# Experts on routed tokens only: slot tiles sorted by expert, rows scattered and results gathered through memory, one image later

## The chip, the cores and the metric

One core of a Trainium2 chip runs the whole program in one launch. TensorE (PE) multiplies matrices, VectorE (DVE) and ScalarE (ACT) work on tiles in the on-chip memory and evacuate PE's results, GpSimd (POOL) issues the indirect DMAs (a DMA whose row addresses come from a list of indices), SyncE (SP) issues the others. Each engine works through its own list of instructions in order and waits on semaphores for the others. The metric is the device time in microseconds (us), the median of the runs.

## What is computed

Eight images of 56 x 56 tokens with 64 channels pass four residual layers. Cut to what matters here:

```python
x = x + conv0(ln(x))        # xn = normalised tokens; y = relu(xn xn^T)^2 (x W), all 3136 x 3136 pairs of an image
t = x + moe(ln(x)):         # 16 experts, 128 hidden units, two per token
    probs = softmax(a @ gate_w + gate_b); top_probs, top_idx = top_k(probs, 2)
    dispatch = sum(one_hot(top_idx) * top_probs / sum(top_probs))
    hidden = silu(a @ w1[e]) * (a @ w2[e])       # the reference: every expert for every token
    out = sum_e (hidden @ w3[e]) * dispatch[e]   # 14 of 16 shares are zero
x = x + deform(ln(x))       # 3x3 deformable convolution: 9 taps, each from 4 corners at learnt offsets
x = x + ffn(x)              # only on the tokens with the largest routing weights (half of each image, less one)
```

## The kernel before, in words

An image's 3136 tokens lie in 25 tiles of 128 (the last has 64) and in 7 chunks of 512 (the last 64). `image(k)` runs through these stages on PE, DVE and ACT: the **mixer** (the layer `conv0`: `sims` multiplies tokens with tokens, ACT's relu and a square on DVE, L777, or ACT follow, `mix` multiplies with the mixed tokens; two halves with 14 steps j in all), then norm and gate (`gate`), then the **dense experts**. There the chunk's 512 tokens go through all 16 experts: `up` (four f16 products, since each weight is held as a high and a low half), a silu on ACT (L1379), `hidden` on DVE (L866), two experts' `down` products, the share of the token spread to channels by another product (`spread`), `scale_pair` (L862), and `collect`, transposes that add the pair to the sum in PSUM. At the end of each chunk the sum goes to the tokens (L884, L888).

Image k-1 is one layer further on beside it. Its deformable convolution takes corners from a table in memory: SP writes the table (`write_table`), and **POOL** walks through the images and their 25 tiles, with nine indirect gathers for each tile (L448: 128 rows of 1024 bytes) into a double buffer G. It waits for the table, for the indices, and until DVE has used the buffer of two tiles before (semaphore `valued`). DVE weighs a tile in five pieces (`weigh`: three products with the corner weights, L486, then two sums, L492 and L494), PE transposes and multiplies it (`sample`), ACT evacuates, DVE adds the result (`sample_add`, L499). Tuples at the top of the file say at which step of the mixer or at which expert a piece goes: ten tiles or so lie beside the mixers, 14 beside the experts, one beside the norm. Image k-2 has its FFN beside the same stages. After the loop come the last image's convolution alone, and the top-k that ranks all tokens.

All products and transposes but those of `sample` go through one helper, `mm`, so they carry its line, L1487.

Of the kernel before, what the change touches and what calls it, by code (L numbers as in the profile page):

```python
# [11 lines left out]
MOE_SAMPLE, MOE_EVAC, MOE_ADD, MOE_WEIGH = (0, 2, 4, 6), (2, 4, 6), 7, (1, 3, 4, 5, 7)  # L12

GEO_EVAC = ((1, 3), (1, 5), (1, 7), (2, 1), (2, 3), (2, 5), (2, 7))
# [5 lines left out]
FFN_EVAC = ((11, 1), (11, 3), (11, 5), (11, 7), (12, 1), (12, 3), (12, 5))  # L20

NORM_DVE, NORM_ACT = (0, 2, 6), (0, 3, 5)


def metaformer_kernel(nc, x, conv_w, gate_w, gate_b, w1, w2, w3, off_w, off_b, dcn_w, wr, br, f1, fb1, f2, fb2,
# [38 lines left out]
    NW = 6  # L64
    ACT_N = len(ACT_STEPS)
# [5 lines left out]
    grid_dram = nc.dram_tensor("grid_scratch", [N, 2 * TAPS], f32).ap()  # L71
    x3_dram = nc.dram_tensor("x3_scratch", [B, N, C], f32).ap()
# [3 lines left out]
    with ctx:  # L76
# [9 lines left out]
        pick = sb("pick", [128, E * C], f16)  # L86
# [8 lines left out]
        w1h = sb("w1h", [128, E * HID], f16)  # L95
        w1l = sb("w1l", [128, E * HID], f16)
        w2h = sb("w2h", [128, E * HID], f16)
        w2l = sb("w2l", [128, E * HID], f16)
# [27 lines left out]
        def routed(flat):  # L126
# [3 lines left out]
        xin_flat, xln_flat, x1_flat, yw_flat = (sb(n, [128, RT * C]) for n in ("xin", "xln", "x1", "yw"))  # L130
        xin, xln, x1, fc = tokens_of(xin_flat), tokens_of(xln_flat), tokens_of(x1_flat), tokens_of(yw_flat)
        yw = routed(yw_flat)
        xm = sb("xm", [TP, T, C])
        tmp = sb("tmp", [TP, T, C])
        xB = [sb(f"xB{q}", [TP, T, C]) for q in range(2)]
        st = sb("st", [TP, 3, 8, T])
        split = sb("split", [TP, T, 4 * C], f16)
        xn_hl = sb("xn_hl", [128, N], f16)
        xn_hh = sb("xn_hh", [128, N], f16)
        xn_ll = sb("xn_ll", [128, N], f16)  # L140
        xf = sb("xf", [128, N], f16)
        dT = xn_hh
# [3 lines left out]
        work = sb("work", [128, max(12 * IWM, 6 * 512 + RT * C)])  # L146
        relu = work[:, 0:4 * IWM].rearrange("p (q b n) -> p q b n", q=2, b=2)
        sq = work[:, 4 * IWM:12 * IWM].rearrange("p (q b n) -> p q b n", q=4, b=2)
        fin_x = (routed(x1_flat), routed(xin_flat))
        fin_y = (work[0:RP, 6 * 512:6 * 512 + RT * C].rearrange("p (t c) -> p t c", c=C), routed(xln_flat))  # L150
        silu = work[:, 0:2 * 512].rearrange("p (q n) -> p q n", q=2)
        hid = work[:, 2 * 512:6 * 512].rearrange("p (q n) -> p q n", q=4)
        small_all = sb("small", [128, 5, 2 * TAPS * T])
# [4 lines left out]
        disp = small[:, 4, 0:T * E].rearrange("p (t e) -> p t e", e=E)  # L158
        dsplit = sb("dsplit", [TP, T, 2 * E], f16)
        om = sb("om", [TP, T, OC])  # L160
        om_cm = sb("om_cm", [128, 512])
# [9 lines left out]
        share = small_flat[:, 0:2 * 512].rearrange("p (q n) -> p q n", q=2)  # L171
        scaled_y = small_flat[:, 2 * 512:4 * 512].rearrange("p (q n) -> p q n", q=2)
        w_all = sb("w_all", [RP, B, RT])

        hit = sb("hit", [RP, NTRY * (B - 1) * RT])
# [21 lines left out]
            logits_done sm_shift sm_exp disp_split disp_tr disp_cm  # L197
            up_done silu_done hid_done share_done share_ready down_done scaled_done ytm_done x2_added
# [5 lines left out]
        gath = (s["gath0"], s["gath1"])  # L204
        BODIES, GROUP = 2 * BPH, 14
        NLATE = T - FULL - 2 * NCH
# [89 lines left out]
        def late_tile(j):  # L296

            return FULL + 2 * NCH + j

        def moe_tile(c, i):  # L300

            return FULL + 2 * c + i

        def token_form(b, t):

            return b == LAST or FULL <= t < FULL + 2 * NCH

        def column_tiles(b, t):

            return b * (T - 2 * NCH) + (t + 1 if t < FULL else t + 1 - 2 * NCH)  # L310
# [3 lines left out]
        def _(sp):  # L314
# [16 lines left out]

            def store_x3(f):
                sp.wait_ge(s["skip_added"], 4 * (f + 1))
                sp.dma_start(whole_tiles(x3_dram[f]), xB[f % 2][:, 0:T - 1, :]).then_inc(s["x3_stored"], 16)
                sp.dma_start(last_tile(x3_dram[f]), xB[f % 2][0:REM, T - 1, :]).then_inc(s["x3_stored"], 16)
# [33 lines left out]
            sp.dma_start(stage3[0:2 * E, 1536:1536 + E * C], pick_in).then_inc(s["w_staged"], 16)  # L369
# [3 lines left out]
            for table in tables:  # L373
                tz = table.rearrange("e n -> (e n)").rearrange("(p n) -> p n", p=128)
                for a in parts:
                    sp.dma_start(tz[:, a:a + 1682], stage[:, 0:1682]).then_inc(s["table_zeroed"], 16)
            sp.wait_ge(s["table_zeroed"], 32 * len(parts))
# [6 lines left out]
            def image(k):  # L384
                if k >= 1:
                    write_table(k - 1)
                if k >= 2:
                    store_x3(k - 2)
                if k + 1 < B:
                    sp.wait_ge(s["x1_added"], 4 * (k + 1))  # L390
                    load_x(k + 1)
                if k >= 2:
                    store_yw(k - 2)

            for k in range(B):
                image(k)
            write_table(B - 1)
            store_x3(B - 2)
            store_yw(B - 2)
# [22 lines left out]
            sp.dma_start(whole_tiles(x3_dram[LAST]), xB[q][:, 0:T - 1, :]).then_inc(s["x3_stored"], 16)  # L422
            sp.dma_start(last_tile(x3_dram[LAST]), xB[q][0:REM, T - 1, :]).then_inc(s["x3_stored"], 16)
# [9 lines left out]
        @block.gpsimd  # L433
        def _(pool):
            pool.wait_ge(s["amax_done"], 1)
            GP.partition_all_reduce(amax_all[:, :], amax[:, :], 128, bass.bass_isa.ReduceOp.max).then_inc(s["amax_red"], 1)

            for b in range(B):
                pool.wait_ge(s["table_written"], (b + 1) * 64)
                for t in range(T):  # L440
                    if t in (0, GROUP):
                        pool.wait_ge(s["idx_ready"], 2 * b + 1 + t // GROUP)
                    n, rows = b * T + t, tile_rows(t)
                    if n >= 2:
                        pool.wait_ge(s["valued"], n - 1)
                    for tap in range(TAPS):
                        col = t * TAPS + tap
                        GP.indirect_dma_start(G[0:rows, n % 2, tap * 4 * C:(tap + 1) * 4 * C], None, tables[b % 2],  # L448
                                              bass.IndirectOffsetOnAxis(ap=index[0:rows, col:col + 1], axis=0)).then_inc(gath[n % 2], 16)
# [3 lines left out]
        def _(dve):  # L453
# [14 lines left out]
            def magnitudes(tensors):  # L468
                for col, src in tensors:
                    red(amax[:, col:col + 1], src, ALU.max)  # L470
                    red(amin[:, col:col + 1], src, ALU.min)
# [25 lines left out]
            def sample_add(b, t):  # L497
                dve.wait_ge(s["dcn_done"], b * T + t + 1)
                V.tensor_tensor(xB[b % 2][:, t, :], xB[b % 2][:, t, :], D0[0:TP, 448:448 + C], ALU.add).then_inc(s["conv_added"], 1)  # L499
# [32 lines left out]
            def split_l(ln, n, half, q):  # L532
                dve.wait_ge(s[ln + "_cast"], 4 * n + q + 1)
                h, r = half * 2 * C, quarter(q)
# [460 lines left out]
            for k in range(B):  # L995
                image(k)
# [926 lines left out]
```

## Time and profile before

| | |
|---|---|
| time, median of 3 runs (lowest to highest) | 4182.69 us (4178.13 to 4189.22) |
| the profiled execution: span | 4742.8 us, clock 0.858 |
| busy in it: PE, DVE, ACT, POOL | 3689.9, 3096.6, 2394.1, 1954.9 us |
| DMA | 314.93 MB in 374811 packets |

The profile's span is the profiled execution's own time as far as it is recorded; it is longer than the runs without the profiler. Busy times of different engines overlap. "Idle before" is the time in which an engine waited ahead of an instruction, and the arrow names what it waited for; "issue" stands for no wait that the profile shows and "remote" for a releaser that it cannot name.

### The profile page before, as it was taken

Reading aid. Unit: us, or ns where it says so; the run is one execution under the profiler, and the core shown is the slowest. Engines: PE = TensorE matmul, PEld = TensorE weight load, DVE = VectorE, ACT = ScalarE, POOL = GpSimd, SP = SyncE. Lnnn points to the kernel's source line nnn. Section 1 sums busy time; section 2 is a strip of 40 time slices with the busy share of each in tenths; the row PEclk is TensorE's granted clock in tenths of the full one; section 3 lists DMA queues with packets and bytes.
Section 4 is the critical chain, followed back from the end, with each engine's and each line's share of the span. In section 5 each row is a group of like instructions: output and inputs, shape, how many; then the busy total and the mean of one; then the engine's idle time right before and its main releaser. Section 6 shows DMA issues by size and latency. Waiting matters only on the chain.

```text
span 4742.8 us, 58643 instructions
## 1 busy us (share of the span) xinstructions
PE 3689.9 (78%) x21912; PEld 1953.7 (41%) x21912; DVE 3096.6 (65%) x4834; ACT 2394.1 (50%) x4144; POOL 1954.9 (41%) x1805
## 2 busy tenths in 40 slices
PE   6889868888788878889788888889788888864432
PEld 2334434444444444444444444444544444433421
DVE  5466457766677566766577567766577576664765
ACT  5656644466445654466445664456444664431210
POOL 0000344526255343535255353544345354446661
PEclk8999979999799978999799888989799988975555
DMA  3000222222122221222122221231222222233436
GB/s 99 8 1 1 73 59 60 65 66 79 51 65 68 70 72 57 67 73 71 51 65 66 70 77 55 64 86 51 55 71 72 71 71 57 60 89 89 111 97 125
DMA packets 374811, 314.93 MB, mean 66 GB/s; under 512 B 312672, under 2 KB 317024, under 8 KB 374528
## 3 DMA queue, kind: packets, MB, share of 16 engines
q0 software_dynamic: 85248, 231.33, 16.5%
q1 hardware_dynamic: 289280, 79.88, 7.9%
q8 instruction: 172, 2.82, 0.2%
q14 instruction: 111, 0.91, 0.1%
HBM read 279.30 MB, written 57.69 MB: 71 GB/s over the span
## 4 chain that ended last, share of the span: by engine, by line
PE 54%; DVE 14%; ACT 9%; another core or an unknown queue 9%; issue 7%; DVEq 3%; DMA 2%; POOL 2%; SPq 1%; ACTq 0%
PE PS L1487 49%; DVE work L866 3%; PE PS L1690 3%; DVEq L488 2%; ACT work L1379 2%; DVE G L492 2%; POOL G L448 2%; PE PS L1522 1%; ACT work L1308 1%; DVE G L486 1%; DVE st L454 1%; DVE small L862 1%; DVE work L777 1%; DMA out<-x 1%
## 5 line engine op out<-in xcount | busy, mean ns | idle before, releaser
L448 POOL DMA_INDIRECT G<-corner_table,index x1800 | 1954.3, 1086 | 2651.6 <-DVE value L494 1256.1
L1379 ACT ACTIVATE work<-PS,descale 128x512 f32<-128x512 f32 (+2 forms) x896 | 565.5, 633 | 638.0 <-PE PS L1487 510.6
L866 DVE SCALAR_TENSOR_TENSOR work<-PS,descale,work 128x512 f32<-128x512 f32 (+2 forms) x896 | 604.8, 681 | 385.0 <-ACT work L1379 276.1
L1308 ACT ACTIVATE work<-PS 128x768 f32<-128x768 f32 (+2 forms) x800 | 650.5, 823 | 374.3 <-PE PS L1487 251.0
L777 DVE TENSOR_TENSOR work<-work 128x768 f32<-128x768 f32 (+2 forms) x496 | 481.1, 973 | 440.2 <-PE PS L1487 280.3
L1487 PE MATMUL PS<-xn_hl,xn_hh 128*128 128x384 f16 (+2 forms) x1600 | 550.8, 345 | 121.8 <-ACT work L1308 76.3
L1487 PE MATMUL PS<-work,xm 128*64 128x400 f32 (+3 forms) x3200 | 642.1, 514 | 0.4 <-DVE work L777 0.4
L486 DVE TENSOR_TENSOR G<-G,corner_w 128x768 f32<-128x768 f32 x600 | 559.8, 951 | 55.9 <-DMA G<-corner_table,index 53.4
L1487 PE MATMUL PS<-xn_hl,xn_ll 128*128 128x384 f16 (+2 forms) x1600 | 546.7, 342 | 0.0
L1487 PE MATMUL PS<-work,w3s 128*64 128x384 f32 (+2 forms) x1792 | 466.8, 600 | 85.6 <-DVE small L862 80.8
L1487 PE MATMUL PS<-xn_hl,w1h 128*128 128x512 f16 (+2 forms) x896 | 331.1, 370 | 157.5 <-DVE work L866 131.3
L1385 ACT ACTIVATE small<-PS 128x512 f32<-128x512 f32 (+2 forms) x448 | 243.0, 542 | 253.1 <-PE PS L1487 195.8
L1487 PEld LDWEIGHTS PS<-xn_hl,xn_hh 128*128 128x128 f16 (+1 forms) x1600 | 160.7, 100 | 461.8 <-ACT work L1308 211.9
L1487 PE MATMUL PS<-xn_hl,w1l 128*128 128x512 f16 (+2 forms) x896 | 329.9, 368 | 0.0
L1487 PE MATMUL PS<-xn_hl,w2h 128*128 128x512 f16 (+2 forms) x896 | 328.3, 366 | 0.0
L1487 PE MATMUL PS<-xn_hl,w2l 128*128 128x512 f16 (+2 forms) x896 | 328.1, 366 | 0.0
L1487 PEld LDWEIGHTS PS<-work,xm 128*64 128x64 f32 (+1 forms) x3200 | 241.3, 139 | 200.8 <-issue 167.2
L862 DVE TENSOR_TENSOR small<-PS,small 128x512 f32<-128x512 f32 (+2 forms) x448 | 276.9, 618 | 55.0 <-PE PS L1487 34.6
L1232 ACT ACTIVATE val_cm<-PS 128x512 f32<-128x512 f32 x200 | 118.3, 592 | 329.0 <-PE PS L1522 241.5
L492 DVE TENSOR_TENSOR G<-G 128x1152 f32<-128x1152 f32 x200 | 271.8, 1359 | 18.1 <-issue 0.4
L1690 PE MATMUL PS<-ident,small 128*128 128x128 f32 x1600 | 262.3, 284 | 2.8 <-issue 1.8
L1337 ACT ACTIVATE work<-work 128x768 f32<-128x768 f32 (+3 forms) x304 | 259.7, 854 | 3.2 <-PE PS L1487 3.1
(258 smaller groups left out, 4959.1 us busy)
## 6 DMA issues: line engine op xcount, KB each, us to landing
G<-corner_table,index POOLq DMA_INDIRECT x1800
corner_table<-rows_scratch SPq DMA_DIRECT2D x32, 784.0 KB
corner_table<-G SPq DMA_DIRECT2D x8, 841.0 KB, 8.5
xin<-x SPq DMA_DIRECT2D x8, 768.0 KB, 5.3
rows_scratch<-xln SPq DMA_DIRECT2D x8, 768.0 KB
x_scratch<-xB SPq DMA_DIRECT2D x8, 768.0 KB
yw_scratch<-yw SPq DMA_DIRECT2D x7, 784.0 KB
x<-x_scratch SPq DMA_DIRECT2D x4, 784.0 KB
```

Of the source, the lines that this page charges most:

```text
L448: GP.indirect_dma_start(G[0:rows, n % 2, tap * 4 * C:(tap + 1) * 4 * C], None, tables[b % 2], bass.IndirectOffsetOnAxis(ap=index[0:rows, c ...
L486: V.tensor_tensor(g, g, bc(w, 2, C), ALU.mult)
L492: V.tensor_tensor(g[:, :, 0:2, :], g[:, :, 0:2, :], g[:, :, 2:4, :], ALU.add)
L777: V.tensor_tensor(sq[0:rows, u % 4, :, 0:n], relu[0:rows, u % 2, :, 0:n], relu[0:rows, u % 2, :, 0:n], ALU.mult).then_inc(s["sq_dve"], 1)
L862: V.tensor_tensor(scaled_y[:, p % 2, 0:w], Y0[:, 0:w], share[:, p % 2, 0:w], ALU.mult).then_inc(s["scaled_done"], 1)
L866: V.scalar_tensor_tensor(hid[:, e % 4, 0:w], S[2 + e % 2][:, 0:w], descale[:, MOE2:MOE2 + 1], silu[:, e % 2, 0:w], ALU.mult, ALU.mult).the ...
L1308: A.activation(relu[0:rows, u % 2, :, 0:n], PS[u % 2][0:rows, :, 0:n], ACT.Relu).then_inc(s["relu_done"], 1)
L1337: A.activation(sq[0:rows, u % 4, :, 0:n], relu[0:rows, u % 2, :, 0:n], ACT.Square).then_inc(s["sq_act"], 1)
L1379: A.activation(silu[:, e % 2, 0:w], S[e % 2][:, 0:w], ACT.Silu, scale=descale[:, MOE1:MOE1 + 1]).then_inc(s["silu_done"], 1)
L1385: A.activation(share[:, e // 2 % 2, 0:w], Y1[:, 0:w], ACT.Copy, scale=1.0 / XS).then_inc(s["share_ready"], 1)
L1487: return P.matmul(o, a, b, start=start, stop=stop, skip_group_check=True)
L1690: ins = P.matmul(D1[0:rows, n * 128:(n + 1) * 128], scaled_y[:, p % 2, n * TP:n * TP + rows], ident[:, :], start=p == 0 and n == 0, stop=p ...
```

## The change

The experts no longer see all tokens. For each image, `positions` (PE) and `route` (DVE) count by products with a triangle of ones where each token stands among those of its expert. Each expert's tokens get whole tiles of 128 **slots**; the 6272 pairs of token and expert need at most 64 tiles. POOL writes each token's row (f16, high and low half) to its two slots in memory (`scatter_rows`, 50 indirect DMAs per image), SP loads the slots, PE works on four slot tiles at a time (16 groups): `turn_over` transposes them, `expert_numbers` reads four expert numbers into PE's registers, `up` and `down` address the weights by them. SP stores the results, POOL gathers them back by token (`gather_results`, 50 indirect DMAs), and `combine` multiplies with the shares and adds. So each layer behind the experts is one image later, and ten units run in place of eight images: unit k has the mixer and gate of image k, the experts of k-1, and the sampling of k-2 and k-3. Behind each mixer come 19 **turns** (8 in the last unit). A turn weighs one tile and samples one; in turns 7 to 15 it also has two groups of slot tiles, and gate, routing, FFN and the next image's norm have turns of their own.

The `sims` products take their stationary operand from a copy that was the moving one, so two copies per image are made instead of three.

The core of the diff, with new functions that it calls:

```diff
+LATE, FIRST, COLUMN = 17, 16, (16, 22)
+
+LATE_WEIGH, LATE_SAMPLE = (7, 8, 9, 10, 11, 12), (0, 8, 9, 10, 11, 12)
+
+SLOTS, TAIL_SLOTS = 19, 8
+
+A_TURN, GATE_TURN, ROUTE_TURN, FFN_TURN, GEO_TURN, NORM_TURN, MOE_TURN, STAT_TURN, STACK_TURN = 2, 3, 5, 3, 6, 5, 7, 16, 16
+
+SCATTERS_FIRST, SCATTERS_PER_TILE = 26, 4
...
+            def load_slots(i):
+                sp.wait_ge(s["scattered"], 2 * T * 16 * (i + 1))
...
-            for b in range(B):
-                pool.wait_ge(s["table_written"], (b + 1) * 64)
+            def gather_tile(b, t):
...
+            def scatter_rows(i, n):
+                t, j = n // 2, n % 2
+                rows = tile_rows(t)
+                GP.indirect_dma_start(slots_dram, bass.IndirectOffsetOnAxis(ap=slot[0:rows, i % 2, j * T + t:j * T + t + 1], axis=0),
+                                      split_a[0:rows, t, :], None).then_inc(s["scattered"], 16)
+
+            def gather_results(i):
+                pool.wait_ge(s["y_stored"], PIECES * 16 * (i + 1))
                 for t in range(T):
...
+                    rows = tile_rows(t)
+                    for j in range(2):
+                        GP.indirect_dma_start(token_y[0:rows, j, t, :], None, y_dram,
+                                              bass.IndirectOffsetOnAxis(ap=slot[0:rows, i % 2, j * T + t:j * T + t + 1], axis=0)
+                                              ).then_inc(s["y_gathered"], 16)
+
+            def unit(u):
+                if valid(u - 2):
+                    gather_results(u - 2)
+                if valid(u - 1):
+                    pool.wait_ge(s["slots_ready"], u)
+                    for n in range(SCATTERS_FIRST if valid(u - 3) else 2 * T):
+                        scatter_rows(u - 1, n)
+                if valid(u - 3):
+                    for t in range(LATE, T):
+                        gather_tile(u - 3, t)
+                        if valid(u - 1):
+                            for n in scatters_after(t):
+                                scatter_rows(u - 1, n)
+                if valid(u - 2):
+                    for t in range(LATE if u - 2 < LAST else T):
+                        gather_tile(u - 2, t)
...
+            def combine(i, step):
+
+                g, x = share[:, i % 2, :, :], xq[i % 4]
+                if step == 0:
+                    dve.wait_ge(s["y_gathered"], 2 * T * 16 * (i + 1))
...
-            def experts_chunk(k, c):
...
+            def route(k):
...
+                tt(c, D1[0:TP, 0:T * E].rearrange("p (t e) -> p t e", e=E), bc(base, 1, T), ALU.add)
+                for j, o in enumerate((o1, o2)):
+                    tt(p, o, c, ALU.mult)
+                    rd(smallc[:, j, :], p, ALU.add)
+                V.tensor_copy(slot[:, k % 2, 0:T], smallc[:, 0, :])
+                V.tensor_copy(slot[:, k % 2, T:2 * T], smallc[:, 1, :]).then_inc(s["slots_ready"], 1)
...
+            def hidden(i, g):
+                n = i * GROUPS + g
+                dve.wait_ge(s["silu_done"], n + 1)
+                V.scalar_tensor_tensor(hid[:, g % 4, :], S[2 + g % 2][:, :], descale[:, MOE2:MOE2 + 1], silu[:, g % 2, :],
+                                       ALU.mult, ALU.mult).then_inc(s["hid_done"], 1)
...
+            def turn(k, r):
...
+                b, t = turn_weigh(k, r)
+                if turn_holds(k, b):
+                    for piece in range(5):
+                        weigh(b, t, piece)
+                b, t = turn_sample(k, r)
+                if turn_holds(k, b):
+                    sample_add(b, t)
...
+                if k < B and r == ROUTE_TURN:
+                    route(k)
...
+                for n in norm_pieces(r):
+                    if k + 1 < B:
+                        norm_piece(k + 1, n)
+                for g in moe_steps(r):
+                    if valid(k - 1) and 1 <= g <= GROUPS:
+                        hidden(k - 1, g - 1)
...
+            def up(i, g):
+
+                pe.wait_ge(s["slot_ready"], i * GROUPS + g + 1)
+                if g >= 2:
+                    pe.wait_ge(s["hid_done"], i * GROUPS + g - 1)
+                experts = expert_numbers(i, g)
+                for n, e in enumerate(experts):
+                    x = slot_cm[:, g % 2, n * TP:(n + 1) * TP]
+                    for h, l, o in ((w1h, w1l, S[g % 2]), (w2h, w2l, S[2 + g % 2])):
+                        mm(o[:, n * TP:(n + 1) * TP], of_expert(h, e), x, True, False)
+                        ins = mm(o[:, n * TP:(n + 1) * TP], of_expert(l, e), x, False, True)
                 ins.then_inc(s["up_done"], 1)
...
+            def of_expert(w, e):
+                return w[:, bass.ds(e, 1), :].rearrange("p a n -> p (a n)")
...
+            def turn(k, r, experts):
+                b, t = turn_sample(k, r)
+                if turn_holds(k, b):
                     for stage in range(4):
...
+                        sample(b, t, stage)
...
+                for g in moe_steps(r):
+                    if valid(k - 1):
+                        if g < GROUPS:
+                            turn_over(k - 1, g)
+                        if 1 <= g <= GROUPS:
+                            experts[g - 1] = up(k - 1, g - 1)
+                        if g >= 2:
+                            down(k - 1, g - 2, experts[g - 2])
```

On POOL's own list, an image before was its tiles in a row (`corner_table0` for even images, `corner_table1` for odd ones, x216 being 24 tiles of nine). Before, at the start:

```order
L436 ISA amax_all<-amax 128x6
L448 DMA G<-corner_table0,index 128x256 x216
L448 DMA G<-corner_table0,index 64x256 x9
L448 DMA G<-corner_table1,index 128x256 x216
L448 DMA G<-corner_table1,index 64x256 x9
```

After, from the end of image 0's tiles on, as one unit follows another (`shared` holds the gathered results, `slot_rows` are the slots in memory):

```order
L548 DMA G<-corner_table0,index 64x256 x9
L548 DMA G<-corner_table1,index 128x256 x153
L562 DMA shared<-slot_results,slot 128x64 x48
L562 DMA shared<-slot_results,slot 64x64 x2
L554 DMA slot_rows<-split_a,slot 8192x128 x26
L548 DMA G<-corner_table1,index 128x256 x9
L554 DMA slot_rows<-split_a,slot 8192x128 x4
```

Seventeen tiles of image 1 (x153, tiles 0 to 16) now have 50 result gathers and 26 scatters between them and its tile 17, and four more scatters follow each of the next tiles.

On PE, two experts of a chunk before, in a later image (`xn_hl` are the chunk's tokens, `w1h` to `w2l` halves of an expert's weights, `work` the hidden units, `pick` the share product, `ident,small` the collecting transposes, `ident,value` the sampling beside):

```order
L1487 MATMUL PS2<-work,w3s 64x512 x2
L1487 MATMUL PS2<-xn_hh,pick 128x512
L1690 MATMUL PS3<-ident,small 128x128 x4
L1487 MATMUL PS0<-xn_hl,w1h 128x512
L1487 MATMUL PS0<-xn_hl,w1l 128x512
L1487 MATMUL PS1<-xn_hl,w2h 128x512
L1487 MATMUL PS1<-xn_hl,w2l 128x512
L1522 MATMUL PS3<-ident,value 128x128 x4
L1487 MATMUL PS0<-xn_hl,w1h 128x512
L1487 MATMUL PS0<-xn_hl,w1l 128x512
L1487 MATMUL PS1<-xn_hl,w2h 128x512
```

After, the sampling at the head of a turn and the beginning of a group, each product with its own expert and 128 columns (`expert_of` holds the expert numbers, the ISA rows set registers, `work` are the slots, turned over):

```order
L1724 MATMUL PS3<-ident,value 128x128 x4
L1728 MATMUL PS3<-ident,value 128x128
L1689 MATMUL PS3<-dcn,val_cm 128x64 x5
L1921 TENSOR_LOAD expert_of
L1689 ISA
L1689 MATMUL PS0<-work,experts_w 128x128
L1689 ISA
L1689 MATMUL PS0<-work,experts_w 128x128
L1689 ISA
```

What had been four products of 512 columns for each of 16 experts is four of 128 columns for each slot tile, with a register instruction ahead of each.

## Rows read from the trace of the kernel before

**Rows 1.** The page: span, and busy time, share and count of each engine.
```profile
span 4742.8 us, 58643 instructions
...
PE 3689.9 (78%) x21912; PEld 1953.7 (41%) x21912; DVE 3096.6 (65%) x4834; ACT 2394.1 (50%) x4144; POOL 1954.9 (41%) x1805
```

**Rows 2.** The page: the chain that ended last, by engine.
```profile
PE 54%; DVE 14%; ACT 9%; another core or an unknown queue 9%; issue 7%; DVEq 3%; DMA 2%; POOL 2%; SPq 1%; ACTq 0%
```

**Rows 3.** Windows (us): width, busy of each engine (instructions), granted clock, DMA share, GB/s.
```profile
56.00:202.00 146.00, 143.66 (x802) 61.38 (x801) 61.97 (x85) 107.28 (x139) 0.00 (x0) 1.00 0.16 51
248.00:436.00 188.00, 174.07 (x903) 76.90 (x904) 121.34 (x207) 105.27 (x178) 0.00 (x0) 0.99 0.00 1
2335.00:2600.00 265.00, 223.46 (x1213) 111.17 (x1213) 199.83 (x304) 127.40 (x232) 132.48 (x126) 0.94 0.23 66
2600.00:2822.00 222.00, 195.36 (x1215) 97.72 (x1215) 134.79 (x192) 143.47 (x242) 102.06 (x90) 0.91 0.27 72
2822.00:2878.00 56.00, 33.13 (x312) 25.94 (x310) 31.45 (x59) 26.17 (x47) 9.15 (x10) 0.68 0.16 41
4268.00:4650.00 382.00, 165.74 (x770) 134.24 (x770) 235.15 (x407) 68.14 (x114) 252.24 (x225) 0.50 0.43 106
4650.00:4743.00 93.00, 17.63 (x77) 13.47 (x77) 53.12 (x147) 6.40 (x10) 0.00 (x0) 0.50 0.52 101
```

**Rows 4.** Groups by line: POOL's gathers (line, engine, operation, count | busy, mean ns | idle before).
```profile
L448 POOL DMA_INDIRECT G<-corner_table,index x1800 | 1954.3, 1086 | 2651.6 <-DVE value L494 1256.1 <-DVE index L667 731.8 <-issue 663.7
```

**Rows 5.** Waits of POOL: line, releaser, us in total, times, longest.
```profile
POOL G L448 <- DVE value L494: 1256.1, 135, 46.9
...
POOL G L448 <- issue: 663.7, 1659, 51.2
```

**Rows 6.** Timeline of POOL, last image: start, us, instruction, idle before.
```profile
4409.97 0.94 POOL L448 DMA_INDIRECT G<-corner_table,index  x1 [0.30 <-issue]
4411.22 3.57 POOL L448 DMA_INDIRECT G<-corner_table,index  x1 [0.30 <-issue]
```

**Rows 7.** Timeline of DVE in the same stretch.
```profile
4411.28 2.69 DVE L486 TENSOR_TENSOR G<-G,corner_w 128x768 f32<-128x768 f32 x3
```

**Rows 8.** Groups by line: three of the dense experts' instructions.
```profile
L866 DVE SCALAR_TENSOR_TENSOR work<-PS,descale,work 128x512 f32<-128x512 f32 (+2 forms) x896 | 604.8, 681 | 385.0 <-ACT work L1379 276.1 <-issue 99.3
...
L1487 PE MATMUL PS<-work,w3s 128*64 128x384 f32 (+2 forms) x1792 | 466.8, 600 | 85.6 <-DVE small L862 80.8 <-issue 2.5 <-DVE work L866 2.2
L1487 PE MATMUL PS<-xn_hl,w1h 128*128 128x512 f16 (+2 forms) x896 | 331.1, 370 | 157.5 <-DVE work L866 131.3 <-issue 17.7 <-ACT xn_hh L1426 7.6
```

**Rows 9.** Groups by line: weight loads and small products, nearest to the new ones.
```profile
L1487 PE MATMUL PS<-dcn,val_cm 128*128 128x64 f32 x1230 | 197.6, 299 | 56.5 <-ACT val_cm L1235 50.9 <-issue 5.7
L1487 PEld LDWEIGHTS PS<-dcn,val_cm 128*128 128x128 f32 x1230 | 189.7, 221 | 87.8 <-ACT val_cm L1235 68.4 <-issue 8.5
...
L1522 PE MATMUL PS<-ident,value 128*128 128x128 f32 x800 | 140.2, 304 | 140.9 <-DVE xB L499 111.5 <-DVE value L494 28.8 <-issue 0.6
...
L1487 PEld LDWEIGHTS PS<-xn_hl,w1h 128*128 128x128 f16 x896 | 96.2, 107 | 224.8 <-DVE work L866 180.0 <-issue 26.3 <-ACT xn_hh L1426 8.7
```

**Rows 10.** Groups by line: DVE work with two inputs in SBUF.
```profile
L486 DVE TENSOR_TENSOR G<-G,corner_w 128x768 f32<-128x768 f32 x600 | 559.8, 951 | 55.9 <-DMA G<-corner_table,index 53.4 <-issue 2.2
...
L777 DVE TENSOR_TENSOR work<-work 128x768 f32<-128x768 f32 (+2 forms) x496 | 481.1, 973 | 440.2 <-PE PS L1487 280.3 <-remote 82.7 <-ACT work L1308 61.1
...
L492 DVE TENSOR_TENSOR G<-G 128x1152 f32<-128x1152 f32 x200 | 271.8, 1359 | 18.1 <-issue 0.4
...
L494 DVE TENSOR_TENSOR value<-G 128x576 f32<-128x576 f32 x200 | 152.2, 761 | 19.0 <-issue 1.3
```

**Rows 11.** Timeline of POOL: a 64-row gather and the next image's first gather.
```profile
4246.99 0.90 POOL L448 DMA_INDIRECT G<-corner_table,index  x1 [0.30 <-issue]
4268.38 1.06 POOL L448 DMA_INDIRECT G<-corner_table,index  x1 [20.49 <-issue]
```

**Rows 12.** Waits of DVE: one line's wait for a releaser that isn't named.
```profile
DVE small L824 <- remote: 74.9, 6, 13.2
```

More of the change, by code:

```diff
@@ L452, in _ @@
+            pool.wait_ge(s["slots_zeroed"], 16 * 2 * PIECES)
+            for u in range(UNITS):
+                unit(u)
         @block.vector
@@ L846, in gate @@
-                V.tensor_tensor(o2, o2, bc(m2, 2, E), ALU.mult)
+                V.tensor_tensor(hot[:, 0:T * E].rearrange("p (t e) -> p t e", e=E), o1, o2, ALU.add).then_inc(s["hot_ready"], 1)
+            def route(k):
+                p, o1, o2, c = routing_views()
+                tiles_f, end, other, base = (ends[:, i, :] for i in range(4))
+                dve.wait_ge(s["pos_done"], k + 1)
+                V.tensor_scalar(counts_i[:, :], D1[0:TP, T * E:(T + 1) * E], float(TP - 1), None, ALU.add)
@@ L956, in _, with unit @@
+            def unit(k):
+                if k < B:
+                    mixer(k)
+                else:
+                    idle_mixer(k)
+                for r in range(turns(k)):
+                    turn(k, r)
             V.memset(table_cell[:, :], 0.0)
@@ L994, in _ @@
             rounds_prepare()
[L995 to L1004 removed]
+            for k in range(UNITS):
+                unit(k)
             def views(b0, nb):
@@ L1434, in _, with unit @@
+            def unit(k):
+                if k < B:
+                    mixer(k)
+                else:
+                    idle_mixer(k)
+                for r in range(turns(k)):
+                    turn(k, r)
             for n in range(6 * NCH):
                 norm_piece(0, n)
-            stacks(0, 0, 3 * NCH)
+            stacks(0, 0, 2 * NCH)
             act.wait_ge(s["w_loaded"], 16 * 16)
             act.wait_ge(s["const_done"], 1)
-            for k in range(B):
-                image(k)
@@ L1441, in _ @@
-            for j in range(BPH):
-                for u in range(SPB):
-                    geo_prepare(LAST, j, u)
-                    for stage in range(3):
-                        if j < NLATE and MIX_EVAC[stage] == u:
-                            sample_evac(PREV, late_tile(j), stage)
+            for k in range(UNITS):
+                unit(k)
             def tail_gelu(f, c):
@@ L1618, in mix, with beside_mixer, idle_mixer @@
                 ins.then_inc(s["mixed"], 1)
+            def beside_mixer(k, j, v):
+                if valid(k - 2):
+                    geo_prepare(k - 2, j - 7, v)
+                if valid(k - 4):
+                    ffn_prepare(k - 4, j, v)
+                for stage in range(4):
+                    if valid(k - 3) and j in LATE_SAMPLE and MIX_SAMPLE[stage] == v:
+                        sample(k - 3, late_sample(j), stage)
+            def idle_mixer(k):
+                for j in range(BODIES):
+                    for v in range(0, steps(j % BPH), 2):
+                        beside_mixer(k, j, v)
             def mixer(k):
@@ new lines, in turn, with unit @@
+                for g in moe_steps(r):
+                    if valid(k - 1):
+                        if g < GROUPS:
+                            turn_over(k - 1, g)
+                        if 1 <= g <= GROUPS:
+                            experts[g - 1] = up(k - 1, g - 1)
+                        if g >= 2:
+                            down(k - 1, g - 2, experts[g - 2])
+                if k + 1 < B:
+                    stacks(k + 1, *stack_turn(r))
+            def unit(k):
+                if k < B:
+                    mixer(k)
+                else:
+                    idle_mixer(k)
+                experts = {}
+                for r in range(turns(k)):
+                    turn(k, r, experts)
@@ L1805, in _ @@
+            stacks(0, 0, 2 * NCH)
             pe.wait_ge(s["w_loaded"], 16 * 16)
@@ L1809, in _ @@
                 mm(bank[:, max(IWS):512], zero16[:, 0:128], zero16[:, 0:512 - max(IWS)])
-            for k in range(B):
-                image(k)
+            for k in range(UNITS):
+                unit(k)
             def count(n, columns):
```

934 lines of the change are left out of this document (481 added, 453 removed).

## The prediction

> **What bounds the kernel now.** First the page's totals: over a span of 4742.8 us PE is busy 78%, DVE 65%, ACT 50%, POOL 41% [rows 1]. No engine is full, so the bound has to be found by stage, and the chain of waits names it: 54% of it is PE, 14% DVE, 2% POOL [rows 2]. Nine per cent of the chain has a releaser that the profile cannot name and 7% none at all; those two, 16% or some 760 us, matter below. Then the windows by stage. With nothing beside it the mixer takes 146 us and the dense experts 188 us of image 0, PE busy 98% and 93% of that. With gathers and sampling beside them they take 265 us (experts, image 4) and 222 us (mixer, image 5), and the norm, gate and FFN between them 56 us: a period of 543 us, which seven images repeat. The last image has its 25 tiles of sampling alone, 382 us at a granted clock of 0.50 (1.2 GHz), and top-k ends 93 us later [rows 3].
>
> Last POOL, whose one kind of instruction decides my forecast. 1800 indirect gathers take 1954.3 us, 1.086 us each, and are late because of the double buffer G or the index, not because POOL is full [rows 4, 5]. Inside one tile they follow at 0.95 us busy plus 0.30 us before the next, 1.25 us from start to start, to the hundredth; one gather lasted 3.57 us, exactly while three L486 multiplies ran on DVE [rows 6, 7]. At the mean a gather costs 1.086 + 0.30 = 1.39 us, a tile of nine 12.5 us, an image's 225 gathers 313 us: 58% of the period. POOL has room for 543 - 313 = 230 us an image.
>
> **What the change removes.** Each image has 112 expert passes over 448 to 512 tokens. Per pass PE does four up products of 0.37 us and two down products of 0.60, and DVE's L866 takes 0.68 [rows 8]. Over 896 passes that is 4 x 331 + 467 = 1791 us of PE and 605 of DVE, beside the share products, the evacuations on ACT and L862. So the whole stage of 265 us goes; its 14 tiles of sampling and the pieces of the next image's norm, which lay beside, stay and go to the new turns.
>
> **What it adds to PE, DVE and ACT.** Sixteen groups of four slot tiles: sixteen products of 128 columns, a quarter of a 512-column row (0.09 us) and each with its own weight load of 0.10 us [rows 9]. Beside each other the two give 16 x 0.10 = 1.6 us, one behind the other 3.1. Four down products, by the nearest f32 row 0.30 us with 0.22 of load, are 1.2 to 2.1; four turning transposes, by the 0.30 of an f32 one, 1.2 at most [rows 9]. A group is 3 to 6.4 us of PE. A turn has two groups and one sampling tile (five transposes by 0.30, five products by 0.30 and loads: 3 to 4.2 us), so 9 to 17 us; DVE has 5.0 us of weighing (3 x 0.95 + 1.36 + 0.76 [rows 10]), two hidden products and three small norm pieces, about 9 us. The register loads of four expert numbers, two per turn, have no row before; they lie between nothing (PE ahead of its inputs) and the 0.30 us of the nearest small f32 row, and I take nothing. For the turn I take the middle, 11 to 13 us: about as long as a tile's nine gathers.
>
> The Trainium skill, DMA: Bandwidth & Descriptors, gives a tensor_load a floor of about 600 ns; no run here shows one. By it the 128 loads would be 77 us of PE, an estimate, and felt only where PE is late.
>
> **What it adds to POOL, which is the term that decides.** Per image 50 scatters and 50 result gathers, so 325 indirect DMAs where there were 225. They have no row of their own: the low end is the undisturbed 1.25 us, the high end 1.43 (below), and 1.39 is the mean of the nearest row, a fair price since they move 128 rows each as the others do, and a gather of 64 rows takes 0.90 us, hardly less [rows 11]. The unit then has 325 x 1.39 = 452 us of POOL in a single queue, in the order gather results, scatter, late tiles, next tiles. Everything else of the unit is shorter: the mixer's 146 us alone, and 19 turns of about 12 us, 228 us, with the norm and gate inside the first of them, are 374 to 430. So the queue becomes the bound, and turns wait on G's nine gathers.
>
> How far DVE holds POOL back changes with that. The extra over 1.25 us is 0.14 us a gather, 252 us in all, while the two-input DVE work of L486, L492, L494 and L777 is 560 + 272 + 152 + 481 = 1465 us: 17% of it is felt with POOL issuing 2502 of 4743 us. If POOL issues nearly always, the share nearly doubles: 1.25 + 0.18 = 1.43 us. I take 1.41.
>
> **The sum, in the profile's own terms.** First tile of image 0: unit 0 has start 56, mixer 146 and turns without experts, 285 in all; unit 1 another 146, 60 of norm and gate and nine turns of 10: about 585; then 50 result gathers (70, the first four of fourteen mixer steps beside them), seven more steps of 10.4 (73), in which offsets and index are made, and the wait for the table, 20 in the tail of now [rows 11]: 748 us. From there 2600 - 150 = 2450 indirect DMAs are still to come: 2450 x 1.41 = 3455. POOL's waits: 40 in unit 2, 20 in each of six units while gate and routing hold DVE, and 60 for the last image's table: 220. After the last gather 94, as before. 748 + 3455 + 220 + 94 = 4517 us against 4742.8: 5% shorter.
>
> **From the profile to the clock.** The profiled execution is 13% longer than the median of 4182.69 us (a factor of 0.882), and the two are not stretched alike. POOL's 0.95 and 0.30 repeat to the hundredth, beside anything and alone, which looks like its own price; DVE's waits of up to 13 us on a releaser that the profile cannot name, 74.9 us in six of them at one line, look like the profiler's [rows 12], and the 760 us of such steps in the chain is more than the 560 us to be explained. If POOL keeps its price, only head, waits and end shrink: 660 + 3455 + 194 + 83 = 4392. If everything shrinks alike, 4517 x 0.882 = 3984. I stand nearer to the first, since part of POOL's 0.14 us of disturbance may be the recorder's: 0.6 x 4392 + 0.4 x 3984 = 4230 us, 1% slower.
>
> **Rivals.**
> - All of it shrinks with the profile, POOL too: 3984 us, 3900 to 4080. For it: 0.30 us between two DMAs with nothing to wait for may be a recorder's. Against: no spread in it, where the recorder's other marks spread by microseconds. Chance 0.27.
> - Slower: the turns set the pace, not POOL. Place: the nine turns with experts, where each product waits for its own register and weights and PE works at a granted clock of 0.5 to 0.7, as it does between the stages and in the tail [rows 3]. At the upper bounds, 17 us and two loads of 0.30, a turn is 17.6, 5.1 over the tile's 12.5; nine turns of seven units are 321 us on top of POOL's time, 4230 + 0.882 x 321 = 4513. It decides from a turn of 12.5 us. For it: the 9 to 17 range; against: loads lie beside products in the rows before. Chance 0.14.
> - Slower too: DVE shuts POOL out for all of its two-input work. Per unit 75 x 0.95 + 25 x 1.36 + 25 x 0.76 + 62 x 0.97 = 184 us; 325 x 1.25 + 184 = 590 us, longer than the 543 of now, and 2450 DMAs at 1.82 give 4459 + 1062 = 5521 in the profile's terms, 4870 shrunk. Against: the mean extra is 0.14 us, 17% of that. Chance 0.04. In the Trainium skill, SBUF — State Buffer, the box on the DVE-blocks-DMA trap and the section behind it (A bandwidth-pool intuition that's wrong) say that POOL writes DMA descriptors through a port pair that it shares with VectorE, that a two-port operation there locks it out meanwhile, and that a DMA of 620 ns then took some 3100 ns. The trace agrees in kind by the 3.57 us gather, and by the mean of 1.086 not in amount.
> - POOL is not the bound because results and scatters cost much less than a gather (their rows are 256 bytes, G's 1024): at 0.6 us a unit is 225 x 1.39 + 60 = 373, the other engines' 400 decide: 748 + 7.5 x 400 + 150 = 3898, shrunk 3440, in part 3700. Against: the 64-row gathers of the last tile cost nearly what the others do [rows 11], so size hardly counts. Chance 0.05.
>
> **How the numbers follow.** The forecast, POOL's queue at its own price, has a chance of 0.50, with 4230 as its time and 4090 to 4400 as its own range. 0.3% is what a measurement of this kernel can tell, so 4170 to 4195 is no change. Of the 0.50, 0.13 falls below, 0.06 within and 0.31 above. The shrinking rival gives 0.26 faster and 0.01 same, the cheap scatters 0.05 faster, the two slower rivals 0.18. Faster 0.44, same 0.07, slower 0.49. The range leaves out the extreme of each side: 3920 to 4520.
>
> **What would show it.** In the profile after: POOL busy well above half the span, its idle time before a DMA mostly 0.3 us, mean 1.05 to 1.13 us; DVE's wait for G grown to many hundred us; PE far below 78%; the granted clock lower in the turns; tiles 12 to 13 us apart in the turns, and units of about 460 us. Wrong, if POOL waits on DVE's value as long as now (turns decide), if the mean of the added DMAs is far from 0.95 to 1.1 us, or if the first gathers come much later than 748 us.

## The result, and the profile after

The kernel after takes 4419.5 us (4413.8 to 4427.3, four runs) against 4183.4 before: ratio 1.057, 95% interval 1.055 to 1.059. It is slower by 5.7%, where 1% was forecast (4230 us), inside the range of 3920 to 4520. The profiled execution is one of the four, 4427.3 us, and this time as long as the others.

The page after: span, busy times, and the chain by engine.

```profile
span 4425.5 us, 51603 instructions
...
PE 2910.2 (66%) x17810; PEld 1891.5 (43%) x17810; DVE 2435.6 (55%) x3747; ACT 1761.2 (40%) x2959; POOL 2925.6 (66%) x2608
...
POOL 43%; PE 23%; issue 13%; DVE 11%; ACT 4%; DMA 3%; DVEq 2%; SPq 1%; ACTq 0%; POOLq 0%
```

POOL went from 41% busy in [rows 1] and 2% of the chain in [rows 2] to 66% and 43%; PE's share of the span fell, and nothing else has become full. POOL's 66% is the whole queue, though: the pause of 0.30 us behind each DMA isn't counted as busy. Groups by line (line, engine, operation, count | busy, mean ns | idle before); L548 answers to L448 in [rows 4], L623 to L486 in [rows 10]:

```profile
L548 POOL DMA_INDIRECT G<-corner_table,index x1800 | 2029.3, 1127 | 681.6 <-issue 537.0 <-DVE value L631 111.8 <-DVE index L822 32.7
...
L623 DVE TENSOR_TENSOR G<-G,corner_w 128x768 f32<-128x768 f32 x600 | 541.5, 953 | 678.2 <-DMA G<-corner_table,index 678.1
...
L554 POOL DMA_INDIRECT slot_rows<-split_a,slot x400 | 485.1, 1213 | 335.1 <-DVE slot L1046 213.5 <-issue 121.5
...
L562 POOL DMA_INDIRECT shared<-slot_results,slot x400 | 410.1, 1025 | 349.5 <-DMA slot_results<-shared 227.8 <-issue 121.7
```

2600 DMAs take 2029 + 485 + 410 = 2924 us, 1.125 each; with the pause 1.425. POOL's waits answer to [rows 5] (us in total, times, longest):

```profile
POOL G L548 <- issue: 537.0, 1762, 0.3
POOL shared L562 <- DMA slot_results<-shared: 227.8, 1, 227.8
POOL slot_rows L554 <- DVE slot L1046: 213.5, 1, 213.5
...
POOL G L548 <- DVE value L631: 111.8, 37, 18.7
```

The wait for DVE's `value`, 1256 us before, is 112. The two large ones are single waits at the start: for the slots of image 0 (213 us) and for its results (228). What waits now is DVE, for G, 678 us (L623 above), where [rows 10] show 53 before. The first and last start of the sampling's gathers (durations as min/median/max):

```profile
L548 POOL DMA_INDIRECT G<-corner_table,index x1800: 897/949/4403, 720.5 to 4331.3; - x180
```

From 720.5 to 4331.3 us POOL issues 2450 DMAs: 2450 x 1.425 = 3491, and 112 of waiting, 3603 of 3611 us. So the span is 720 us of filling, a queue that hardly pauses, and 94 us at the end.

Where the other engines of a unit wait for the queue is seen on POOL's timeline at the start of unit 7, beside the last mixer (start, us, instruction, idle before): the last gather of image 4's tile 16, then 50 result gathers, 26 scatters, and the first gather of tile 17.

```profile
2870.36 0.95 POOL L548 DMA_INDIRECT G<-corner_table,index  x1 [0.30 <-issue]
2871.61 0.95 POOL L562 DMA_INDIRECT shared<-slot_results,slot  x1 [0.30 <-issue]
...
2938.81 0.91 POOL L562 DMA_INDIRECT shared<-slot_results,slot  x1 [0.30 <-issue]
2940.03 1.00 POOL L554 DMA_INDIRECT slot_rows<-split_a,slot  x1 [0.30 <-issue]
...
2980.27 1.07 POOL L554 DMA_INDIRECT slot_rows<-split_a,slot  x1 [0.31 <-issue]
2981.64 0.98 POOL L548 DMA_INDIRECT G<-corner_table,index  x1 [0.30 <-issue]
```

Tile 16 is done at 2871 and tile 17 begins at 2982, 110 us later. DVE comes to tile 17's weighing in the mixer's middle and waits, with the mixer's squares (L951) queued behind:

```profile
2979.51 0.98 DVE L951 TENSOR_TENSOR work<-work 128x800 f32<-128x800 f32 x1
2994.49 1.83 DVE L623 TENSOR_TENSOR G<-G,corner_w 128x768 f32<-128x768 f32 x2 [13.99 <-DMA G<-corner_table,index]
```

### The profile page after: what moved, and what is told of

Its sections match the earlier page's. It is cut to its first block, busy times and chain, and to the rows that moved or that the text cites. A ratio compares the mean times of both kernels' runs of the same rounds, so it can differ in the third digit from the quotient of the medians.

```text
span 4425.5 us, 51603 instructions
## 1 busy us (share of the span) xinstructions
PE 2910.2 (66%) x17810; PEld 1891.5 (43%) x17810; DVE 2435.6 (55%) x3747; ACT 1761.2 (40%) x2959; POOL 2925.6 (66%) x2608
## 4 chain that ended last, share of the span: by engine, by line
POOL 43%; PE 23%; issue 13%; DVE 11%; ACT 4%; DMA 3%; DVEq 2%; SPq 1%; ACTq 0%; POOLq 0%
POOL G L548 28%; PE PS L1689 22%; POOL shared L562 9%; POOL slot_rows L554 6%; DVE G L623 2%; DMA G<-corner_table,index 2%; DVE G L629 1%; DMA out<-experts_w 1%; DVEq L625 1%; DVE small L972 1%; DVE value L631 1%; PE PS L1724 1%; DVE st L590 1%; ACT small L1551 0%; DVE smallc L590 0%
## 5 line engine op out<-in xcount | busy, mean ns | idle before, releaser
L548 POOL DMA_INDIRECT G<-corner_table,index x1800 | 2029.3, 1127 | 681.6 <-issue 537.0
L623 DVE TENSOR_TENSOR G<-G,corner_w 128x768 f32<-128x768 f32 x600 | 541.5, 953 | 678.2 <-DMA G<-corner_table,index 678.1
L1689 PE MATMUL PS<-xn 128*128 128x400 f16 (+3 forms) x3200 | 647.9, 346 | 236.0 <-ACT work L1515 229.8
L951 DVE TENSOR_TENSOR work<-work 128x768 f32<-128x768 f32 (+2 forms) x496 | 479.7, 973 | 457.0 <-PE PS L1689 415.3
L554 POOL DMA_INDIRECT slot_rows<-split_a,slot x400 | 485.1, 1213 | 335.1 <-DVE slot L1046 213.5
L562 POOL DMA_INDIRECT shared<-slot_results,slot x400 | 410.1, 1025 | 349.5 <-DMA slot_results<-shared 227.8
L1689 PEld LDWEIGHTS PS<-xn 128*128 128x128 f16 (+1 forms) x3200 | 289.8, 101 | 666.4 <-ACT work L1515 389.2
L1689 PE MATMUL PS<-dcn,val_cm 128*128 128x64 f32 x1580 | 349.5, 378 | 57.9 <-ACT val_cm L1426 57.9
L1689 PEld LDWEIGHTS PS<-dcn,val_cm 128*128 128x128 f32 x1580 | 331.1, 297 | 85.5 <-ACT val_cm L1426 85.5
L629 DVE TENSOR_TENSOR G<-G 128x1152 f32<-128x1152 f32 x200 | 271.7, 1358 | 15.8 <-issue 0.4
L1689 PE MATMUL PS<-work,experts_w 128*128 128x128 f16 x2048 | 259.8, 280 | 12.5 <-issue 11.7
L1689 PEld LDWEIGHTS PS<-work,experts_w 128*128 x2048 | 209.7, 120 | 54.0 <-issue 23.0
L1689 PE MATMUL PS<-w3s,work 128*128 x1024 | 214.2, 379 | 21.2 <-DVE work L1058 21.0
L1689 PEld LDWEIGHTS PS<-w3s,work 128*128 128x128 f32 x1024 | 196.4, 286 | 33.1 <-issue 26.0
```

Source lines behind the costliest of these rows:

```text
L554: GP.indirect_dma_start(slots_dram, bass.IndirectOffsetOnAxis(ap=slot[0:rows, i % 2, j * T + t:j * T + t + 1], axis=0), split_a[0:rows, t, ...
L562: GP.indirect_dma_start(token_y[0:rows, j, t, :], None, y_dram, bass.IndirectOffsetOnAxis(ap=slot[0:rows, i % 2, j * T + t:j * T + t + 1], ...
L623: V.tensor_tensor(g, g, bc(w, 2, C), ALU.mult)
L629: V.tensor_tensor(g[:, :, 0:2, :], g[:, :, 0:2, :], g[:, :, 2:4, :], ALU.add)
L951: V.tensor_tensor(sq[0:rows, u % 4, :, 0:n], relu[0:rows, u % 2, :, 0:n], relu[0:rows, u % 2, :, 0:n], ALU.mult).then_inc(s["sq_dve"], 1)
L1689: return P.matmul(o, a, b, start=start, stop=stop, skip_group_check=True)
```

## The experiments

Theory A: POOL's queue is the bound of the kernel after, each indirect DMA costs about 1.43 us there whatever it moves, with or without the profiler, and the profile of before that I forecast from was stretched. Theory B: POOL's cost shrinks without the profiler, and the loss is in the turns, the ten units or the addressed weights. All kernels below but the last were timed once, in the profiled execution itself, so only differences far above 0.3%, the spread of the four runs of the kernel after, are read from them.

**The kernel before, recorded once more.** No edit.

> The kernel before, unchanged, profiled a second time. Its first profile had a span of 4743 us against 4183 without the profiler, while the kernel after shows 4426 against 4419. Theory A (the stretching is a property of recording this kernel, above all of PE's many instructions, and repeats): span again 4650 to 4800, with DVE and ACT waits on unnamed releasers of 200 us and more. Theory B (one bad recording): span near 4200, and then POOL's 0.95 and 0.30 us stand in it unchanged.

Measured: 4193.4 us, span 4191.6. The second of its theories held: the first recording was longer than the runs by 13%, this one isn't. The page of the second recording (span, busy, chain by engine):

```profile
span 4191.6 us, 58643 instructions
...
PE 3546.0 (85%) x21912; PEld 1920.7 (46%) x21912; DVE 3088.6 (74%) x4834; ACT 2401.7 (57%) x4144; POOL 2003.0 (48%) x1805
...
PE 60%; DVE 16%; ACT 9%; issue 4%; POOL 4%; DVEq 4%; DMA 2%; SPq 1%; ACTq 0%
```

The releaser without a name, 9% of the chain in [rows 2], is gone. Windows of the second recording, columns as in [rows 3]: mixer and experts of image 0 with nothing beside, then experts (image 4) up to the next mixer, then mixer with norm, gate and FFN (image 5).

```profile
56.00:202.00 146.00, 144.08 (x791) 61.46 (x791) 60.97 (x82) 106.14 (x138) 0.00 (x0) 0.98 0.16 51
249.00:437.00 188.00, 173.82 (x900) 76.64 (x901) 121.00 (x207) 105.76 (x179) 0.00 (x0) 0.99 0.00 1
2069.00:2296.00 227.00, 209.15 (x1213) 108.08 (x1213) 198.80 (x303) 128.19 (x231) 129.07 (x124) 0.98 0.26 75
2296.00:2539.00 243.00, 224.88 (x1525) 128.55 (x1526) 166.20 (x253) 169.73 (x289) 117.16 (x102) 0.90 0.29 77
```

The stages without gathers beside them are the same in both recordings, 146 and 188 us. Those with gathers took 265 and 222 + 56 = 278 us in [rows 3] and take 227 and 243 here: the period that the runs have is 470 us and not 543 (456 to 473 from an image's first tile to the next one's, up to image 6). POOL's line is nearly as it was in [rows 4], 1112 ns for 1086:

```profile
L448 POOL DMA_INDIRECT G<-corner_table,index x1800 | 2002.4, 1112 | 2052.0 <-DVE value L494 729.1 <-DVE index L667 686.0 <-issue 636.8
```

So POOL's price was read rightly and PE's stages were not. What stretched the first recording, the profiler or something else in that one execution, isn't known; it didn't recur in the other recordings that have runs to compare with (this one, the kernel after, the last experiment), and it wasn't tried further.

**Dense experts, with idle gathers added to POOL's queue.**

```diff
+                    for m in range(EXTRA_N if b < LAST else 0):      # EXTRA_N = 8
+                        if n:
+                            pool.wait_ge(extras[m], 16 * n)
+                        GP.indirect_dma_start(extra[0:rows, m, :], None, x.rearrange("b h w c -> (b h w) c"),
+                                              bass.IndirectOffsetOnAxis(ap=extra_i[0:rows, m:m + 1], axis=0)).then_inc(extras[m], 16)
```

> The kernel before with the dense experts as they were, and eight idle indirect gathers of 128 rows of 256 bytes behind each tile of images 0 to 6 (1400 in all, into a tile that nobody reads). Theory A (POOL's queue is the bound of the kernel after, and an indirect DMA costs 1.43 us there and here, with or without the profiler): 3200 DMAs in one queue from about 480 us on, 480 + 3200 x 1.43 + 94 = 5150 us, up to 5300 with waits. Theory B (the kernel after is slow by its turns, its ten units or its addressed weights, and an indirect DMA without the profiler costs 1.1 us or less): 480 + 3200 x 1.1 + 94 = 4090, so no more than 4183 to 4400.

Measured: 5195.3 us, 1011 more than before for 1400 DMAs. POOL's waits there, and its two groups of DMAs:

```profile
POOL G L455 <- issue: 662.1, 1781, 20.1
POOL G L455 <- DVE index L679: 483.0, 1, 483.0
POOL extra L460 <- issue: 426.7, 1400, 0.3
POOL G L455 <- DVE value L506: 69.6, 18, 7.9
```

```profile
L455 POOL DMA_INDIRECT G<-corner_table,index x1800 | 1921.6, 1068 | 1214.6 <-issue 662.1 <-DVE index L679 483.0 <-DVE value L506 69.6
L460 POOL DMA_INDIRECT extra<-x,extra_i x1400 | 1493.8, 1067 | 426.7 <-issue 426.7
```

POOL waits 70 us for DVE after its start, so its queue is the bound of this kernel as well, with all of the old experts and none of the new units. Theory A holds against B, which had nothing above 4400. That the time is within 1% of A's 5150 is partly luck. A DMA cost 1.367 us here (1.067 and the pause) and not 1.43, which is 200 us less on 3200 of them. A first gather at 527 us in place of 480, the 70 us for DVE and another 128 us in gaps of up to 20 us (662.1 - 1781 x 0.30), none of which the 5150 holds, made up for it.

**The kernel after without result gathers, and without scatters as well.**

```diff
             def gather_results(i):
                 pool.wait_ge(s["y_stored"], PIECES * 16 * (i + 1))
-                for t in range(T):
...
-                dve.wait_ge(s["y_gathered"], 2 * T * 16 * (i + 1))
+                dve.wait_ge(s["y_stored"], PIECES * 16 * (i + 1))
```

and in the second kernel `scatter_rows` is empty, with the waits for its DMAs put on `slots_ready`. So `combine` adds whatever lies in the results' tile, and in the second kernel the slots hold zeros; all other work is done.

> The kernel after without its 400 result gathers (combine adds what lies in the slots' tile in place of the tokens' results). Theory A (POOL's queue): 400 x (1.025 + 0.30) = 530 us less, 3890; up to 4000 if the other engines' path of a unit is longer than POOL's 275 x 1.43 = 393 us. Theory B (turns, units): 4300 to 4420.

> The kernel after without its 400 result gathers and without its 400 scatters; slots hold zeros, all else is done on them. Theory A: POOL's 225 x 1.43 = 322 us per unit are no longer the bound; the other engines' path of a unit, 374 to 430 us by the prediction's terms, is: 3450 to 3800 us, and POOL waits on DVE's value again by hundreds of us. Theory B (turns, units): 4300 to 4420.

Measured: 4055.9 us (364 less than after) and 3992.8 (427 less). Neither theory is right alone. POOL was the bound, since the first 400 DMAs bring 0.91 us each; but not all of their 1.33, and the next 400 bring only 63 us. POOL's wait for DVE's `value` in the first and its two largest waits in the second say why:

```profile
POOL G L548 <- DVE value L625: 230.0, 44, 22.6
```

```profile
POOL G L548 <- DVE index L813: 661.2, 1, 661.2
POOL G L548 <- DVE value L622: 601.9, 67, 75.2
```

112 us has become 230 and 602: POOL has room again, and the other engines' path of a unit, forecast at 374 to 430, now sets the pace. In the second kernel the first tiles of images 0 to 5 follow each other at 415 to 429 us; the 661 us are the wait for the first index, at the start. Even if moving rows had cost POOL nothing, the kernel would have come to 3993, 4.6% below before.

**DVE's products left out.** `weigh` without its three multiplications (L623), in the kernel after.

```diff
-                    V.tensor_tensor(g, g, bc(w, 2, C), ALU.mult)
+                    pass
```

> The kernel after without DVE's 600 two-input products in weigh (L623); the sums behind them stay. Theory A (those products shut POOL out while it writes descriptors): the gather's mean falls from 1.13 us to about 1.0, 1800 x 0.13 and a little on scatters and results, 220 to 300 us less, 4120 to 4200. Theory B (the extra over 0.95 us has another cause, such as memory traffic): POOL's means as before, and since POOL's queue is the bound, 4380 to 4420 although DVE has 541 us less to do.

Measured: 4223.2 us, 196 less. POOL's groups:

```profile
L548 POOL DMA_INDIRECT G<-corner_table,index x1800 | 1866.6, 1037 | 653.8 <-issue 541.0 <-DVE value L631 80.1 <-DVE index L822 32.7
L554 POOL DMA_INDIRECT slot_rows<-split_a,slot x400 | 478.8, 1197 | 334.8 <-DVE slot L1046 213.3 <-issue 121.5
L562 POOL DMA_INDIRECT shared<-slot_results,slot x400 | 401.2, 1003 | 349.4 <-DMA slot_results<-shared 227.8 <-issue 121.6
```

The gather fell from 1.127 to 1.037 us, 1800 x 0.090 = 162, and 15 more from the others. POOL's wait for `value` fell by another 32. So the products do lengthen POOL's DMAs, a little less than theory A said (220 to 300 us). Over all 2600 DMAs the excess over 0.95 us was 455 us and is 277: 39% of it went with these products, which are 541 of the 1445 us of DVE's two-input work (L623, L629, L631 and L951). That it is the writing of descriptors that they hold up is not shown here: without them DVE also reads and writes less of G. The Trainium skill, SBUF — State Buffer, in its box on the DVE-blocks-DMA trap and the section behind it, has a DMA issued by POOL take five times as long beside a two-port operation of DVE. The runs agree that DVE can hold such a DMA up, here beside products with two inputs in SBUF; on the mean of 1800 gathers it is 1.127 us against 1.037, 9%.

**Three taps in place of nine.** The second kernel above, with three gathers for each tile from the third on.

```diff
-                for tap in range(TAPS):
+                for tap in range(3 if n >= 2 else TAPS):
```

> The kernel after without its result gathers and scatters, and with three gathers for each tile from the third on in place of nine (the other taps' corners are stale). A tile costs POOL 4.2 us in place of 12.8. Theory A (with the moves gone, the 19 turns are still paced by a tile's nine gathers, since the double buffer lets POOL run only two tiles ahead, while POOL idles in the mixer): a turn falls from 12.8 to some 9 us, 70 us a unit, 3400 to 3600. Theory B (turns take 12 us or more by PE, ACT and DVE themselves): 3850 to 3990.

Measured: 3735.5 us, between the two. The first and last `value` of image 3's tiles 0 to 16, so 16 turns, in the kernel after, without moves, and with three taps:

```profile
L631 DVE TENSOR_TENSOR value<-G x17: 757/759/759, 2177.3 to 2397.8; 128x576 f32<-128x576 f32 x17
```

```profile
L622 DVE TENSOR_TENSOR value<-G x17: 758/758/759, 2007.4 to 2219.0; 128x576 f32<-128x576 f32 x17
```

```profile
L622 DVE TENSOR_TENSOR value<-G x17: 757/758/760, 1933.0 to 2134.5; 128x576 f32<-128x576 f32 x17
```

16 turns take 220.5, 211.6 and 201.5 us: 13.8, 13.2 and 12.6 each. With a tile that costs POOL 4 us a turn is still 12.6, so the turns are that long by PE, ACT and DVE themselves, and theory A's 9 us was wrong. Of the 257 us, 165 came behind image 5's first tile, where the two units that are left have no mixer.

The 12.6 us are a mean of unlike turns: by the starts of `value` with three taps, turns 3 to 5, which hold gate, FFN and routing, take 16 to 26 us, and the nine with experts 11.7 on the mean. In these nine (2011 to 2116 us) PE is busy 87 of 105 us at a granted clock of 0.65, where the dense experts in the window from 2069 us of the second recording had 0.98; what a turn would take at the higher clock was not tried. The loads of the expert numbers, which had no row before, have one in the kernel after (durations in ns):

```profile
L1921 PEldq TENSOR_LOAD <-expert_of x128: 328/332/1129, 483.6 to 3757.2; - x128
```

They sum to 56 us in 4425, and the trace names no engine that waited for one.

**One part of the change alone.** The kernel before with two copies of the normalised tokens for `sims`.

```diff
-                    mm(o, xn_hh[:, j * TP:j * TP + rows], xn_hl[:, i:i + n], True, False)
-                    ins = mm(o, xn_ll[:, j * TP:j * TP + rows], xn_hl[:, i:i + n], False, True)
+                    mm(o, xn_hl[:, j * TP:j * TP + rows], xn_hl[:, i:i + n], True, False)
+                    ins = mm(o, xn_hl[:, j * TP:j * TP + rows], xn_ll[:, i:i + n], False, True)
```

(with `xn_ll` now the low half above the high, 14 chunk transposes for 21, and `xn_hh` set to zero once)

> The kernel before with only one small part of the change: two copies of the normalised tokens for the similarity products in place of three. Seven chunk transposes and seven ACT copies of 0.6 us less per image between the experts and the next mixer, and half of DVE's low-half subtraction: if that stretch is on the path, 4 to 6 us an image, 4140 to 4155; if it is hidden, no change.

Measured: 4162.6 us, ratio 0.9957 (0.9941 to 0.9972) to before. 0.4% less, 22 us and not the 29 to 44 expected, so a part of the stretch was hidden. It is the fastest of the kernels here that compute everything.

## Why the prediction was right and wrong

- **POOL's queue becomes the bound**: right. 1.41 us per DMA was forecast, 1.425 measured; the added ones cost 1.213 (scatter) and 1.025 (results) plus 0.30, on the mean 1.42 where the nearest row had 1.39. Units of 452 us in the queue were forecast; 325 x 1.425 are 463, and with POOL's waits the first tiles of images 1 to 5 follow each other at 471 to 486.
- **The sum in the profile's terms**: 748 + 3455 + 220 + 94 = 4517 forecast, 720 + 3491 + 112 + 94 = 4417 measured, 2% over: POOL's waits were sized 108 us too long and the filling 28, the DMAs 36 too short.
- **A turn of 11 to 13 us**: right for the turns with experts, 11.7 with POOL out of the way; 12.6 on the mean of 16 turns there, and 13.8 in the kernel after. Addressed weights and register loads are no burden that shows: the loads took 56 us in all.
- **From the profile to the clock**: this is the step that failed. "I stand nearer to the first", 0.6 x 4392 + 0.4 x 3984, gave a weight of 0.4 to the whole sum shrinking by 0.882. Nothing of it shrank: 4427.3 us in the profiled execution, 4413.8 to 4423.9 in the three others. The reason given, that a part of POOL's 0.14 us of disturbance may be the recorder's, failed as well: the second recording, which isn't stretched, has 0.16 (1.112 us). The factor belonged to one recording, and there to stages that had gathers beside them: image 4's experts were 77 us longer than image 0's [rows 3], and the second recording leaves 39 of that. The first of the two sums, 4392, was 0.6% off; its head, waits and end, shrunk to 937, stood for 926 by luck, the waits having been sized too long.
- **The rival that all shrinks**, chance 0.27, is refuted by the three other runs of the kernel after, which keep the queue's full length, and by the idle gathers in the dense kernel: 1400 of them cost 1011 us.
- **Where the gain went**, against the second recording of before (4425.5 - 4191.6 = 234 us). The first tile is weighed at 758.0 in place of 557.6 us: 200 later, with the two extra steps through memory and the lag by an image; POOL's moves are 17 of these, since the first tile is still weighed at 741.2 without them. From there to the first tile of image 7, 4004.1 - 758.0 = 3246 against 3762.9 - 557.6 = 3205: 41 more, or 464 us a unit against 458. From there to the end it is 421 against 429. The sparse experts took out some 40 us per unit of the other engines' path (415 to 429 without moves, against 456 to 473), and POOL's hundred DMAs put them back.

The 200 us are read from the traces and not from a run of their own.

One reading ahead of the prediction was off without weight in the sum: the chunks are 512, 448 and 384 tokens wide, by the forms of the up products, and not 512 with a last one of 64, nor 448 to 512.

## What to carry to other kernels

Count the indirect DMAs before anything else: at 128 rows each cost the issuing engine 1.25 to 1.43 us in these kernels, so a change that trades PE work for them must fit into the time that this queue has left. Here that was 464 - 313 = 151 us per image for 100 DMAs of 1.43: they just fit, and with the queue full there was nothing left for PE's saving to shorten. A profiled span that differs from the runs by 13% is a recording to be taken again, or at least to be read stage by stage against a stage with nothing beside it, before a factor is applied to any sum. And a pipeline that gets one stage longer pays for its filling once, at the start, whatever the stages save later.

## What the hardware showed that I had not expected

A gather of 256-byte rows costs POOL what one of 1024 bytes does (0.95 us undisturbed, both), and a scatter the same (0.96); 64 rows cost 0.90. The price is per DMA and hardly per row or byte.

The disturbance by DVE grew as the prediction had it, though the mean of one gather hides it: 1.112 us in the second recording of before, 1.127 in the kernel after. In the prediction's terms, the excess over 0.95 us as a share of DVE's two-input work, it is 292 of 1467 us, 20%, with POOL issuing 61% of the span, and 455 of 1445, 31%, with 84%, spread over 2600 DMAs in place of 1800. The dense kernel with idle gathers is a little off that line, with 375 of 1467 us, 26%, at 84%.
